# Layers 1 to 3 of the last unit but one behind the last unit's products, and the last pairs in the room of the one-hot rows

## The reference

```python
e = jnp.stack([tbl_0[ids[:, 0]], ..., tbl_25[ids[:, 25]]], axis=1)
combined = jnp.concatenate([e, r_dense_x[:, None, :]], axis=1)
z = jnp.einsum('bfd,bgd->bfg', combined, combined)[:, _TRIU_I, _TRIU_J]
h = jnp.concatenate([z, r_dense_x], axis=1)
h = jnp.maximum(h @ W_top1 + b_top1, 0.0)   # 479 -> 512
h = jnp.maximum(h @ W_top2 + b_top2, 0.0)   # 512 -> 256
y = h @ W_top3                              # 256 -> 1
```

## Time and profile before

| | us |
|---|---|
| median of 3 runs (lowest, highest) | 380.98 (380.67, 381.51) |
| profiled execution's own time | 381.93 |
| its span, first to last instruction | 379.9 |
| TensorE busy | 333.2 |
| VectorE, ScalarE, GpSimd busy | 247.8, 203.5, 252.2 |

### The profile page before, as it was taken

The page is one execution under the profiler, slowest core; times in us unless marked ns, Lnnn a source line. Parts: engine busy times, 40 slices in busy tenths (PEclk is TensorE's granted clock), DMA queues, the critical chain, the costliest instruction groups (busy, mean ns, idle before and its releaser), DMA issues.

```text
span 379.9 us, 9782 instructions
## 1 busy us (share of the span) xinstructions
PE 333.2 (88%) x4178; PEld 315.5 (83%) x4178; DVE 247.8 (65%) x298; ACT 203.5 (54%) x274; POOL 252.2 (66%) x262
## 2 busy tenths in 40 slices
PE   0687649969999999989998999989998999899647
PEld 0587539869899998989898989989898989898545
DVE  3979804995479745994489547973599538952113
ACT  2476375525755466645844575635654585457312
POOL 2888777777777777777777777777777777720000
PEclk9999987999999999999999999999999999999959
DMA  6995423463254623553255425452356225310310
GB/s 254 388 311 146 97 55 105 125 167 77 57 143 106 178 60 94 141 174 84 64 150 148 124 55 146 106 162 72 87 144 179 77 59 155 84 29 2 84 40 0
DMA packets 32377, 44.92 MB, mean 118 GB/s; under 512 B 18791, under 2 KB 20463, under 8 KB 32334
## 3 DMA queue, kind: packets, MB, share of 16 engines
q1 hardware_dynamic: 23080, 25.82, 23.9%
q0 software_dynamic: 8192, 16.79, 16.9%
q10 hardware_dynamic: 1062, 1.69, 1.2%
HBM read 38.07 MB, written 6.20 MB: 117 GB/s over the span
## 4 chain that ended last, share of the span: by engine, by line
PE 53%; DVE 24%; POOL 10%; issue 8%; DMA 4%; ACT 0%; SPq 0%; ACTq 0%; DVEq 0%
DVE hot L650 21%; PE ps_gram L428 15%; PE ps_mix L446 11%; POOL emb L372 10%; PE ps_feat L410 7%; PE ps_feat L411 7%; PE ps_feat L396 5%; PE ps_mix L480 4%; PE ps_feat L446 2%; DMA idx<-in_ids 1%; PE ps_mix L485 1%; DMA products_dram<-gram 1%; DVE h_l L686 1%; PE ps_mix L495 1%; DVE z_l L692 1%
## 5 line engine op out<-in xcount | busy, mean ns | idle before, releaser
L372 POOL DMA_INDIRECT emb<-in_tbl,idx x256 | 251.6, 983 | 83.0 <-issue 76.2
L650 DVE TENSOR_TENSOR hot<-ids_row,ps_rows 128x1024 fp32r<-128x1024 int32 x160 | 186.1, 1214 | 22.0 <-PE ps_feat L411 17.8
L410 PE MATMUL ps_feat<-hot,held_h 128*128 128x256 f32 x640 | 163.3, 294 | 16.6 <-DVE held_l L636 11.3
L558 ACT COPY feat<-ps_feat 128x512 f32<-128x512 f32 x104 | 125.7, 1227 | 76.8 <-PE ps_feat L396 46.0
L411 PE MATMUL ps_feat<-hot,held_l 128*128 128x256 f32 x640 | 158.5, 285 | 0.0
L410 PEld LDWEIGHTS ps_feat<-hot,held_h 128*128 128x128 f32 x640 | 123.9, 194 | 19.1 <-issue 17.0
L411 PEld LDWEIGHTS ps_feat<-hot,held_l 128*128 128x128 f32 x640 | 124.2, 194 | 0.0
L428 PEld LDWEIGHTS ps_gram<-feat 128*54 128x54 f32 x2048 | 56.8, 134 | 9.5 <-issue 5.3
L428 PE MATMUL ps_gram<-feat 128*54 128x54 f32 x2048 | 61.8, 219 | 0.8 <-ACT feat L558 0.8
L396 PE MATMUL ps_feat<-ident,emb 128*128 128x128 f32 x256 | 40.3, 281 | 8.3 <-DMA emb<-in_tbl,idx 8.3
L580 ACT ACTIVATE h_h<-ps_mix,b_sb 128x256 fp32r<-128x256 f32 x29 | 13.8, 475 | 52.4 <-DVE h_x L700 52.0
(11 more groups left out here) (78 smaller groups left out, 250.1 us busy)
## 6 DMA issues: line engine op xcount, KB each, us to landing
ids_row<-in_ids_h SPq DMA_DIRECT2D x40, 256.0 KB, 4.4
products_dram<-gram SPq DMA_DIRECT2D x30, 189.0 KB
held_raw<-in_held SPq DMA_DIRECT2D x8, 512.0 KB, 12.5
emb<-in_tbl,idx POOLq DMA_INDIRECT x256
z_raw<-products_dram SPq DMA_DIRECT2D x93, 26.0 KB
held_raw<-in_held ACTq DMA_DIRECT2D x2, 512.0 KB, 8.6
dense<-in_dense_t SPq DMA_DIRECT2D x8, 128.0 KB
w1z_raw<-in_W_top SPq DMA_DIRECT2D x3, 234.0 KB
```

Of the source, the lines that this page charges most:

```text
L372: pool.indirect_dma_start(emb[:, h, f, :], None, table, bass.IndirectOffsetOnAxis(ap=idx[:, i * UNIT + h, f:f + 1].bitcast(u32), axis=0),) ...
L410: nc.tensor.matmul(dst, held_h[:, o, c, :], hot[:, n % 2, c, :], start=c == 0, stop=False)
L558: nc.scalar.copy(feat_v[:, f, b], src).then_inc(act_out, 1)
L650: nc.vector.tensor_tensor(hot[:, n % 2, chunks, :], bass.AP(ids_row, (n % SLOTS) * UC, [[SLOTS * UC, HR], [0, PC], [1, UC]]), row_nums[:, ...
```

## The change

Only the last unit and what follows it change. Of the layers of the last unit but one, just block 0 of layer 1 stays in the last unit, behind table 9 (place 0.95). Blocks 1 to 3, layer 2, the weighing and layer 3 (`HELD_BACK`) come behind the last unit's products, on TensorE ahead of the last unit's dense chunk, its layer 3 behind the last unit's layer 1. On ScalarE the three activations of layer 1 stand between its stores and its loads, the two of layer 2 behind its loads. The last unit's pairs, dense parts, the weighed sums and a second `y` get tiles of their own in the room of `hot` (`late`), so the loads of the pairs wait for the tables (`hot_used`) and not for layer 2. The last unit's banks are dealt anew, the last layer 1 goes block by block, and the y store of unit 6 goes from ahead of the last product stores to the end of SP's queue.

```diff
+    HELD_BACK = [("l1", n) for n in range(1, N1)] + [("l2", n) for n in range(N2)]
-    def steps(later):
+    def steps(later, last=False):
...
-        l1 = [("l1", n) for n in range(N1)] if later else []
-        l2 = [("l2", n) for n in range(N2)] + [("weigh", 0)] if later else []
-        l3 = [("l3", 0)] if later else []
+        l1 = [("l1", n) for n in range(1 if last else N1)] if later else []
+        l2 = [("l2", n) for n in range(N2)] + [("weigh", 0)] if later and not last else []
+        l3 = [("l3", 0)] if later and not last else []
...
-                           (l1, 0.62, 1)):
+                           (l1, 0.9 if last else 0.62, 1)):
...
+        late = {}
+        late_at = placed_at["hot"]
+        for name, shape, dt in (("z_raw", [ZR, ZC, UC], fp32), ("z_h", [ZR, ZC, UC], f32r), ("z_l", [ZR, ZC, UC], f32r),
+                                ("den_h", [128, S, GROUPS], f32r), ("den_l", [128, S, GROUPS], f32r),
+                                ("weigh", [128, 2, UC], fp32), ("y", [1, UC], fp32)):
+            late[name] = nc.alloc_sbuf_tensor_at("late_" + name, shape, dt, offset=late_at)
+            late_at += 4 * math.prod(shape[1:])
...
-        last_bank = {("l1", 0): (ps_feat, 0), ("l1", 1): (ps_feat, 1), ("l1", 2): (ps_feat, 2), ("l1", 3): (ps_mix, 0),
-                     ("l2", 0): (ps_mix, 1), ("l2", 1): (ps_gram, 0), ("l3", 0): (ps_gram, 1)}
+        last_bank = {("l1", 0): (ps_feat, 0), ("l1", 1): (ps_feat, 1), ("l1", 2): (ps_feat, 2), ("l1", 3): (ps_gram, 0),
+                     ("l2", 0): (ps_gram, 1), ("l2", 1): (ps_mix, 1), ("l3", 0): (ps_rows, 0)}
```

SP, in `products_through_dram` and its loop over the units:

```diff
-                reached(sp, l2_done, i * N2)
+                if is_last(i):
+                    sp.wait_ge(hot_used, UNITS * NH)
+                else:
+                    reached(sp, l2_done, i * N2)
...
-                if i > 0:
+                if i > 0 and not is_last(i):
                     store_y(i - 1)
                 products_through_dram(i)
+            store_y(UNITS - 2)
             store_y(UNITS - 1)
```

TensorE, behind the last unit:

```diff
             j = UNITS - 1
+            for kind, k in HELD_BACK:
+                later(j - 1, kind, k)
+            products_out(pe, (j + 1) * BATCHES - 1)
+            products_out(pe, (j + 1) * BATCHES - 2)
             pe.wait_ge(dense_low, j + 1)
-            pe.wait_ge(y_made, j)
             for n in range(N1):
                 l1_chunk(j, n, 0)
-            pe.wait_ge(z_low, j * ZC + 1)
             for n in range(N1):
-                l1_chunk(j, n, 1)
-            for n in range(N1):
-                for c in range(1, ZC):
+                for c in range(ZC):
                     if n == 0:
                         pe.wait_ge(z_low, j * ZC + c + 1)
                     l1_chunk(j, n, c + 1)
-            products_out(pe, (j + 1) * BATCHES - 1)
-            products_out(pe, (j + 1) * BATCHES - 2)
+            later(j - 1, "l3", 0)
+            pe.wait_ge(h2_made, j * N2)
             for n in range(N2):
                 later(j, "l2", n)
```

ScalarE, behind the last unit:

```diff
             store_products(act, UNITS - 1, range(S // 2, S))
+            for kind, k in HELD_BACK:
+                if kind == "l1":
+                    later(UNITS - 2, kind, k)
             act.wait_ge(gram_stored, UNITS * S * 16)
             load_pairs(act, UNITS - 1, slice(3, None))
+            later(UNITS - 2, "l2", N2 - 1)
             for c in range(ZC):
                 later(UNITS - 1, "z", c)
```

VectorE, behind the last unit:

```diff
+            for kind, k in HELD_BACK:
+                if kind == "l1":
+                    later(UNITS - 2, kind, k)
             for c in range(ZC):
                 later(UNITS - 1, "z", c)
+            later(UNITS - 2, "weigh", 0)
             for n in range(N1):
                 later(UNITS - 1, "l1", n)
+            later(UNITS - 2, "l3", 0)
             later(UNITS - 1, "l3", 0)
```

More of the change, by code:

```diff
@@ L3 @@
 from contextlib import ExitStack
+import math
 def diagonals(features):
@@ L103, in steps, with is_last @@
         return found + [("parts", 0)] + merged((gram[HALF:], 0, 1), (l3, 0, 0.1), (following[PIECES:], 0, 1))
+    def is_last(j):
+        return j == UNITS - 1
     order = steps(False)
@@ L160, in dlrm_tower_kernel @@
         hot = sb("hot", [HR, 2, HC, UC], f32r)
+        late = {}
[5 more added lines that the diff above has]
+            late_at += 4 * math.prod(shape[1:])
+        assert late_at <= placed_at["hot"] + 4 * 2 * HC * UC
         held_h = sb("held_h", [HR, NH, HC, D], f32r)
@@ L244, in copied_out @@
                 reached(eng, act_out, i * NA + act_nth[bank] + 1)
-        def is_last(j):
-            return j == UNITS - 1
-        last_bank = {("l1", 0): (ps_feat, 0), ("l1", 1): (ps_feat, 1), ("l1", 2): (ps_feat, 2), ("l1", 3): (ps_mix, 0),
-                     ("l2", 0): (ps_mix, 1), ("l2", 1): (ps_gram, 0), ("l3", 0): (ps_gram, 1)}
+        last_bank = {("l1", 0): (ps_feat, 0), ("l1", 1): (ps_feat, 1), ("l1", 2): (ps_feat, 2), ("l1", 3): (ps_gram, 0),
+                     ("l2", 0): (ps_gram, 1), ("l2", 1): (ps_mix, 1), ("l3", 0): (ps_rows, 0)}
         mix = {("l1", 0): 0, ("l1", 1): 1, ("l1", 2): 0, ("l1", 3): 1, ("l2", 0): 0, ("l2", 1): 1, ("l3", 0): 0}
@@ L283, in feature_bank, with z_of, dense_of, weigh_of @@
             return dense[:].unsqueeze(1), slice(DENSE, DENSE + 1), slice(0, UC)
+        def z_of(j):
+            return (late["z_raw"], late["z_h"], late["z_l"]) if is_last(j) else (z_raw, z_h, z_l)
+        def dense_of(j):
+            return (late["den_h"], late["den_l"]) if is_last(j) else (den_h, den_l)
+        def weigh_of(j):
+            return late["weigh"] if j == UNITS - 2 else h1_x
+        def y_of(j):
+            return late["y"] if j == UNITS - 2 else y
         def dense_cols():
@@ L302, in load_pairs @@
                     at = (i % 2) * S * FR * F * GROUPS + (row * (F + 1) + d) * GROUPS
-                    eng.dma_start(z_raw[p:p + rows, c, :],
+                    eng.dma_start(z_of(i)[0][p:p + rows, c, :],
                                   bass.AP(products_dram, at, [[(F + 1) * GROUPS, rows], [FR * F * GROUPS, S], [1, GROUPS]])
@@ L337, in store_y @@
                 sp.wait_ge(y_made, j + 1)
-                sp.dma_start(out[:, j * UC:(j + 1) * UC], y[:]).then_inc(y_out, 16)
+                sp.dma_start(out[:, j * UC:(j + 1) * UC], y_of(j)[:]).then_inc(y_out, 16)
             load_ids_rows(0, 0)
@@ L441, in l1_chunk @@
                 if c == 0:
-                    terms = three(w1d_h[:, n], w1d_l[:, n], den_h[:, :, :], den_l[:, :, :])
+                    terms = three(w1d_h[:, n], w1d_l[:, n], *(part[:, :, :] for part in dense_of(j)))
                 else:
-                    terms = three(w1z_h[:, c - 1, n], w1z_l[:, c - 1, n], z_h[:, c - 1, :], z_l[:, c - 1, :])
+                    terms = three(w1z_h[:, c - 1, n], w1z_l[:, c - 1, n], *(part[:, c - 1, :] for part in z_of(j)[1:]))
                 for m, term in enumerate(terms):
@@ L494, in later @@
                     pe.wait_ge(weighed, j + 1)
-                    nc.tensor.matmul(bank_of(j, kind, k)[0:1, :], ones[:], h1_x[:, 1, :], start=True, stop=True
+                    nc.tensor.matmul(bank_of(j, kind, k)[0:1, :], ones[:], weigh_of(j)[:, 1, :], start=True, stop=True
                                      ).then_inc(l3_done, 1)
             def unit(i):
-                for kind, k in steps(i > 0):
+                for kind, k in steps(i > 0, is_last(i)):
                     if kind == "rows":
@@ L560, in dense_part @@
             def dense_part(i):
-                reached(act, l1_done, i * N1)
-                nc.scalar.copy(den_h[:], dense_cols()).then_inc(dense_high, 1)
+                if is_last(i):
+                    act.wait_ge(hot_used, UNITS * NH)
+                else:
+                    reached(act, l1_done, i * N1)
+                nc.scalar.copy(dense_of(i)[0][:], dense_cols()).then_inc(dense_high, 1)
             def products(i, b):
@@ L574, in later @@
                     act.wait_ge(z_in[k], 16 * len(CHUNKS[k]) * (j + 1))
-                    reached(act, l1_done, j * N1)
-                    reached(act, weighed, j)
-                    nc.scalar.copy(z_h[:, k, :], z_raw[:, k, :]).then_inc(z_high, 1)
+                    if not is_last(j):
+                        reached(act, l1_done, j * N1)
+                        reached(act, weighed, j)
+                    raw, high, _ = z_of(j)
+                    nc.scalar.copy(high[:, k, :], raw[:, k, :]).then_inc(z_high, 1)
                 elif kind == "l1":
@@ L663, in dense_part @@
                 dve.wait_ge(dense_high, i + 1)
-                nc.vector.tensor_tensor(den_l[:], dense_cols(), den_h[:].bitcast(fp32), ALU.subtract
+                high, low = dense_of(i)
+                nc.vector.tensor_tensor(low[:], dense_cols(), high[:].bitcast(fp32), ALU.subtract
                                         ).then_inc(dense_low, 1)
@@ L676, in weigh @@
                 dve.wait_ge(h2_made, (j + 1) * N2)
```

(14 more changed lines are left out.)

## The result

The changed kernel takes 376.02 us (median of 4, 375.79 to 377.17) against 380.83 us (380.37 to 381.51) beside it: ratio 0.988, 95% interval [0.986, 0.991]. It is 4.8 us faster where 8.0 were forecast, and its time lies 0.2 us above the stated range. The profiled execution took 375.79 us, its span is 373.8.

The account below looks back on a forecast made before the run. TensorE was taken to bound the last unit and idle right behind it. Terms 6.96 + 1.1 − 0.05 gave 8.0 us, a forecast of 373.0 us; stated range 371.9 to 375.8.

Parts of the forecast that it names:

- first term: Last unit up to its products' end and stores: with work held back, these come 6.96 us earlier.
- ScalarE's rounds: Last unit: ScalarE's feature copies run at 1.525 us a round after block 0's activation.
- the wait on rows 7: Before the last four batches: TensorE waits 0.99 us for ScalarE's copy, bounds 0 and 0.99.
- the last pair chunk decides: Tail: the last pair chunk's split, 6.15 us after the loads as before, sets the pace, now at 361.11.
- rival 2: Tail: ScalarE's six pair loads are held behind the third held-back activation, 0.6 us to spare; e.g. 373.9 us; chance 0.08.
- I take full clock: Tail: TensorE keeps full clock through 3.1 us of waits; the other bound is 28 matmuls at 0.215, 2.7 us.
- Rival 1: Tail: TensorE's clock falls in the shorter wait, 2.7 us more, 375.7 us, less where late; chance 0.26.
- the wait before the first chunk: Tail: TensorE waits about 1.3 us between the dense block and the first pair chunk.
- no single wait is now over 1.4 us: Tail: sign against a clock fall, TensorE's longest single wait being 358.0 to 359.3.
- the kept-back layer 3: Behind the last layer 1: its 0.52 us on TensorE fits into 0.57 left, but for some 0.05 of restarts.

Follow-up runs that it names:

- n = 32: 32 one-column products, results unchanged, added at TensorE's start to the changed kernel, shifting its instruction packets: 371.62 us, ratio [0.973, 0.980].
- n = 64: 64 one-column products, one whole 16 KB instruction packet, added at TensorE's start to the changed kernel: 373.78 us, ratio [0.978, 0.986].
- n = 128: 128 one-column products, two whole instruction packets, added at TensorE's start to the changed kernel: 375.96 us, one execution.

## Why the prediction fell short

- **The first term held.** The stores are issued 7.94 us earlier than before (356.37 to 348.43); less the 0.72 from ahead of the change that is 7.2, against 6.96. The difference is in ScalarE's rounds, which ran at 1.41 us (338.85 to 343.09 in three), not 1.525; the wait on rows 7 is 0.52 in place of 0.99, but 0.2 of that went to TensorE's rounds, which came later than counted.
- **The step that failed first:** "the last pair chunk decides: before it was split 6.15 us after the loads (...), now at 361.11". It took over the loads' duration from a tail in which TensorE stood still. With the work that the change puts beside them, TensorE's last instruction packet falls 1.7 us behind the first load and no longer among the stores: 7.58 us, 1.43 more; with the packet moved away (n = 32) it is 5.97. The row was there, in the middle units of the trace before, and I had read only medians of the issues. Of rival 2 nothing came true: ScalarE's third activation ended 0.6 us ahead of its loads, as counted; it was the loads themselves that stood.
- **The step that failed second:** "I take full clock". Rival 1 came true, at half its price: 14 matmuls at 0.213 in place of 0.119, 1.3 us (1.38 with the slow start behind the split), and not 28. The two steps hang together in part: the standstill made the wait before the first chunk 2.41 us where I had 1.3. But the prediction would have failed here without it: with the loads at 3.70 us and first waits of 1.25 and 1.18 us (n = 32 and n = 64), as short as forecast, the clock still fell, for 3.4 us. The sign that I held against rival 1, "no single wait is now over 1.4 us", was the wrong one; what kept the clock up was matmuls in the waits or 12 behind the first. The Trainium skill (TensorE: Matmul & The Clock Gate, section HAM oscillation) names waits on transfers between bursts as what sends the clock back; the runs agree that they do, with 2.41 us and a fall here, but the wait alone doesn't decide, with no fall after 2.50 us where the burst behind it had 12 matmuls instead of 3.
- **The rest held.** From the last layer-1 matmul to the end 7.25 us (366.55 to 373.8) against 7.21, the kept-back layer 3 hidden but for 0.15. The sum of the misses, 1.43 + 1.38 + 0.04 − 0.26 = 2.6 us, is the 8.0 forecast less the 5.4 of the profiles without the 0.72. This account is of the two profiled executions, 381.93 and 375.79; the medians lie only 4.8 apart, as the first was 1.1 us above its median and the second 0.2 below, and no trace was kept of the other executions. The forecast's upper end was short because it priced the clock and not the loads.
- The order of the last layer 1 cost more than the 9 matmuls that I counted: 2.5 us with the clock that it lost.

Open: the runs with n = 32 on the changed kernel came about 4 us under it in whole time (371.6 against 375.5 and 376.0), while the profiled stretch explains 1.5; its profiled execution was the slowest of its six (374.6). Whether in the others the clock stayed up isn't to be seen.

## What to carry to other kernels

When work is moved into a gap, ask what else was absent in the gap: the engine's own instruction packets, and the load they put on the transfers that the gap was waiting for. Read the longest issue of a line, not only its median, also in units where little waits for it. And where an engine must wait for pieces, give it all the work of the first piece as it arrives, and of the next as far as the next engine's chain allows: here the first piece shortened the end and kept the clock up, and the second, taken the same way, cost 1.0 us.

## What the runs showed of the hardware

- A 16 KB packet of TensorE's instructions that meets a stream of 256-byte packets can hold up the issue of both queues for 0.8 to 1.4 us (the loads' 3.70 us against 4.51 to 5.14 in six traces; in one of them, n = 128, SP's queue alone, as ScalarE was already issuing its last load). The last stores of the kernel before stood still in the same way. I read it so that the next load isn't issued while pieces of those ahead of it wait behind the packet; no run shows that. The Trainium skill (DMA: Bandwidth & Descriptors, section Queues, rings and completion order) has SP's and ScalarE's queues as rings on the same 16 engines; the trace agrees so far as both stood still at once.
- Which packet of the run it is decides whether it does: the 18th and the 34th never did (6 meetings), the others in 32 of 33.
- The granted clock fell to 0.50 after a wait of 2.41 us and two bursts of 3 matmuls, and also after one of 1.18 us and 6 matmuls; after waits of 2.50 and 1.18 us with 12 matmuls in a row behind them it stayed at 1.00.
